# A graph network's adjacency build on one core: the prologue reordered, count masks in bf16, node features loaded and split earlier

## The chip, the cores and the metric

The kernel runs on one core of a Trainium2 chip. The metric is the time of one execution in microseconds of device time, the median over several runs. The engines are TensorE (PE in the rows; PEld is its weight load), VectorE (DVE), ScalarE (ACT), GpSimd (POOL) and SyncE (SP), which issues most DMAs. Each engine works through its own instructions in order and waits on semaphores for the others.

## The reference

Four graph layers follow one another on 3125 nodes with 128 features and 53125 edges sorted by destination; each ends in a residual sum and a layer norm. The change touches what goes before the first one and the walk that the other three use:

```python
src = jnp.concatenate([_s, _d, _loop])
dst = jnp.concatenate([_d, _s, _loop])
_o = jnp.argsort(dst, stable=True)
...
for l in range(N_LAYERS):                      # first graph layer, 4 rounds
    agg = jax.ops.segment_sum(x[src], dst, num_segments=n)
    h = x + agg
    h = jnp.maximum(h @ W1[l] + b1[l], 0.0)
    x = h @ W2[l] + b2[l]
```

## The kernel before

**Stages.** The kernel turns the edge list into a dense matrix `adj` (nodes by nodes, counts in bf16), so that the four rounds of `segment_sum` become matmuls (the dense layers). The other three graph layers gather rows by edge with indirect DMAs (the gather passes). The stages stand one after the other: prologue, build of `adj`, dense layers, tables and gather passes.

**Prologue.** The edges are cut into 416 tiles of 128. The *fine walk* has 620 steps, each a pair of a tile and a block of 16 destination nodes that it reaches; the *coarse walk* has 440 steps over blocks of 128. VectorE loads the last destination of each tile (`tmax`), compares it with a row of step numbers (`fcmp_m`, `cmp_m`, L1587 and L1588), and TensorE counts the ones with a matmul against `ones` (L929, L932): that gives each step's tile (`fts_f`, `ts_f`). From them VectorE makes selection masks (`fsel_m`, `sel_m`, L1597 and L1600), with which TensorE picks the tiles' destinations and sources (L937, L945); these become `drel`, and the comparison keys `fkey` and `flow`. VectorE further works out, on one partition, the place of each step's sum and of its ring slot for the gather passes (`walk_i`, L1605 to L1616), the slots of the fine sums (`fslot_i`), the step at which each block ends (`ends_f`, turned by TensorE, L951, and read by ScalarE into `ends_i`), and a number `peak_i` which every engine loads and branches on: zero (always here) leads to the dense path. GpSimd's part are constants and a check on the coarse walk (`off_f`, and the copies `gwalk`, L767 to L772), for which VectorE waits before it sets `ends_ready`. L957 and L958 join sources and edge kinds into `tile8` and `tile16`.

**Build.** TensorE clears its eight banks (L971), waits for `peak_set`, branches, and runs 31 iterations of four groups of five fine steps. For each group VectorE writes one-hots (`fine_hots`: one L1676, five L1680; two buffers, so at most two groups ahead), TensorE multiplies them (L1001), and ScalarE copies each finished block of 16 columns into `adj` and clears its slot (`copy_out`, L1379 and L1383). From iteration 6 on TensorE adds to each group a part of the first round's sums over the features (L985), 20 iterations with 15 such matmuls each. In these iterations it needs `x3`, the node features as a sum of three bf16 parts.

**Features.** `features_in_parts` on GpSimd (L886 to L900) makes `x3` from seven chunks of `x`, four instructions a chunk (the last is a quarter). It stands behind the branch on `peak_i`, and so do the DMAs of `x` (SyncE, L639 to L642), which land in columns of `adj` that the build reaches late (`xlate`, `xrem`). TensorE waits for them block by block in the first of its sums (`xparts_set`).

**Order.** Everything stands in the order in which it is written. In VectorE's code `link` adds a semaphore wait behind an instruction whose result the next needs. `walk_i` is read only in the gather passes, `gwalk` only where `peak_i` is above zero.

## Time and profile before

| | us |
|---|---|
| median of 3 runs | 2730.95 (2728.96 to 2734.68) |
| the profiled execution, its own time | 2718.4 |
| its span, first to last instruction | 2716.5 |
| prologue, to the first L1001 | 0 to 74.57 |
| build, 31 iterations | 74.57 to 356.59 |

Mean granted TensorE clock of the span: 0.726. A row of the timeline gives start, duration, engine, line, operation, what is written and read, partitions x elements, a count of merged instructions, and in brackets how long the engine was idle before and what released it. An f32 matmul stands in the rows as two.

### The profile page before, as it was taken

What the parts mean: (1) busy time and instruction counts of PE and PEld (TensorE: products, weight loads), DVE (VectorE), ACT (ScalarE), POOL (GpSimd) and SP (SyncE); (2) the same over time, 40 slices, a digit from 0 to 9 for tenths busy, and PEclk for the clock granted to TensorE, in tenths of its full rate; (3) what the DMA queues carried; (4) which work ended last, traced back from release to release, by engine and by line L of the source; (5) the groups of instructions that cost most, each with busy time, mean ns of one, the idle gap of its engine ahead of it and who ended that gap; (6) DMA issues with size and microseconds to landing.
All of it is one profiled execution on the core that took longest, in us unless ns stands there. A gap on an engine that the chain in (4) does not pass through costs nothing.

```text
span 2716.5 us, 30629 instructions
## 1 busy us (share of the span) xinstructions
PE 1369.1 (50%) x6416; PEld 878.8 (32%) x6417; DVE 913.9 (34%) x2288; ACT 657.2 (24%) x1868; POOL 1353.2 (50%) x1570
## 2 busy tenths in 40 slices
PE   4578789999852444543453243443344223233323
PEld 3244344554432332332331232332233123122323
DVE  6777731211276222222233232322234012111212
ACT  0567720000121222332231233333334000000000
POOL 1300045303136666666644666666662756666665
PEclk8699999999885766766776566666767556565656
DMA  0000010000341222322222122222221211111111
GB/s 18 25 0 0 0 11 8 6 0 7 110 185 47 93 78 92 96 77 92 94 81 77 43 69 67 70 59 67 70 67 58 51 42 51 48 49 45 50 46 43
DMA packets 120575, 148.92 MB, mean 55 GB/s; under 512 B 74731, under 2 KB 88689, under 8 KB 117314
## 3 DMA queue, kind: packets, MB, share of 16 engines
q0 software_dynamic: 40000, 81.89, 11.6%
q1 hardware_dynamic: 80514, 66.31, 7.4%
q8 instruction: 27, 0.44, 0.1%
q14 instruction: 34, 0.28, 0.0%
HBM read 91.39 MB, written 56.72 MB: 55 GB/s over the span
## 4 chain that ended last, share of the span: by engine, by line
PE 33%; another core or an unknown queue 30%; issue 17%; DVE 10%; ACT 5%; DVEq 1%; POOL 1%; DMA 1%; ACTq 1%; SPq 0%; POOLq 0%
PE acc L1123 12%; PE acc L1270 9%; PE acc L1236 4%; PE acc L1001 3%; ACT adj L1460 3%; DVE feat L1680 2%; PE acc L1206 2%; DVE adj L1875 1%; ACT adj L1379 1%; POOL adj L837 1%; PE acc L1055 1%; PE acc L985 1%; DVE adj L1944 1%; DVE feat L1676 1%
## 5 line engine op out<-in xcount | busy, mean ns | idle before, releaser
L837 POOL DMA_INDIRECT adj<-table,adj x1248 | 1196.1, 958 | 724.9 <-issue 362.2
L1270 PE MATMUL acc<-adj 128*128 x2640 | 477.0, 346 | 457.5 <-issue 220.3
L1270 PEld LDWEIGHTS acc<-adj 128*128 128x128 f32 x2640 | 434.7, 252 | 514.4 <-issue 513.3
L1123 PE MATMUL acc<-adj,feat 128*128 (+1 forms) x1800 | 337.0, 348 | 2.2 <-DVE adj L1715 2.2
L1875 DVE TENSOR_TENSOR adj<-acc,drel 128x768 f32<-128x768 f32 (+1 forms) x148 | 138.6, 945 | 456.5 <-remote 304.2
L787 POOL TENSOR_TENSOR node_rep<-node_rep,compb 128x128 f32<-128x128 f32 x128 | 58.4, 456 | 464.6 <-DMA node_rep<-in_L_gnn_weight_dram 455.8
L1460 ACT ACTIVATE adj<-adj 128x128 f32<-128x128 f32 x832 | 259.3, 387 | 100.1 <-issue 70.1
L1223 PE MATMUL acc<-ident,adj 128*128 128x128 f32 x50 | 22.0, 439 | 487.4 <-DVE adj L1914 383.4
L1236 PE MATMUL acc<-adj 128*128 128x512 f32 (+2 forms) x400 | 201.7, 660 | 98.4 <-ACT adj L1475 67.9
L1443 ACT ACTIVATE adj<-feat 128x4 int32 (+1 forms) x196 | 34.2, 202 | 882.3 <-remote 635.0
L1123 PEld LDWEIGHTS acc<-adj,feat 128*128 (+1 forms) x1800 | 156.1, 98 | 176.3 <-issue 3.6
L1001 PE MATMUL acc<-feat 128*128 128x400 bf16 x620 | 143.3, 371 | 83.2 <-DVE feat L1680 33.8
L1223 PEld LDWEIGHTS acc<-ident,adj 128*128 128x128 f32 x50 | 8.6, 172 | 497.6 <-issue 301.2
L1680 DVE TENSOR_SCALAR feat<-feat,temp 128x400 bf16<-128x400 int16 x620 | 163.6, 330 | 0.0
L1236 PEld LDWEIGHTS acc<-adj 128*128 128x128 f32 x400 | 94.9, 265 | 188.1 <-issue 117.7
L1896 DVE TENSOR_TENSOR adj<-acc,adj 128x128 f32<-128x128 f32 x75 | 21.7, 289 | 332.4 <-remote 282.9
L1666 DVE TENSOR_TENSOR adj<-node_iob,drel 128x384 f32<-128x384 bf16 (+1 forms) x148 | 74.9, 551 | 171.6 <-remote 130.8
L1001 PEld LDWEIGHTS acc<-feat 128*128 128x128 bf16 x620 | 75.0, 121 | 155.9 <-issue 141.2
L1379 ACT ACTIVATE adj<-acc 128x400 f32 (+1 forms) x196 | 96.5, 493 | 86.2 <-PE acc L1001 82.0
L1443 ACT ACTIVATE adj<-tile 128x4 int32 (+1 forms) x98 | 17.6, 201 | 360.4 <-remote 306.1
L1383 ACT ACTIVATE acc<-zerob 128x400 f32<-128x400 bf16 x196 | 99.5, 508 | 18.0
L1676 DVE TENSOR_TENSOR feat<-node_rep,feat 128x640 bf16<-128x640 bf16 x124 | 74.1, 598 | 75.4 <-PE acc L1001 66.1
(262 smaller groups left out, 1149.6 us busy)
## 6 DMA issues: line engine op xcount, KB each, us to landing
table<-adj SPq DMA_DIRECT2D x50, 512.0 KB
table<-adj SPq DMA_DIRECT2D x25, 1024.0 KB
adj<-table,adj POOLq DMA_INDIRECT x1250
table<-adj SPq DMA_DIRECT2D x25, 64.0 KB
adj<-in_x_dram SPq DMA_DIRECT2D x3, 512.0 KB, 6.4
out_dram<-adj SPq DMA_DIRECT2D x24, 64.0 KB
wrel<-node_rep SPq DMA_DIRECT2D x16, 64.0 KB, 3.0
adj<-in_L_gnn_W_dram SPq DMA_DIRECT2D x2, 512.0 KB
```

The costliest lines, as they stand in the source:

```text
L837: pool.indirect_dma_start(ring[:, p_, 0:D], None, table, bass.IndirectOffsetOnAxis(ap=gidx[:, p_:p_ + 1], axis=0)).then_inc(msgs_in[u.r][c ...
L1001: nc.tensor.matmul(acc[:, bass.ds(places[q * FG + j], FCOLS)], flo[:, q % FBUF, :, j], foh[:, q % FBUF, j, :], start=False, stop=True, ski ...
L1123: last = nc.tensor.matmul(acc[:, c * KB:c * KB + chunk(c)], x3[:, s, bass.ds(b, 1), :].rearrange("p b f -> p (b f)"), adj[:, bass.ds(b, 1) ...
L1236: nc.tensor.matmul(o, xT1[:, b.r, :], table, start=True, stop=True).then_inc(prod_full[j], 1)
L1270: last = nc.tensor.matmul(acc[:, bass.ds(blk[s], width)], hot[:, c, j, :], ring_flat[:, bass.ds(place[s], width)], start=False, stop=True, ...
L1379: nc.scalar.activation(adj[:, :, bass.ds(i * (TURN * FB) + r * FB, FB)], fslots[r % FSLOTS].rearrange("p (h n) -> p h n", n=FB), ACT.Copy) ...
L1383: nc.scalar.activation(fslots[r % FSLOTS], zerob[:, 0:FCOLS], ACT.Copy).then_inc(zeroed, 1)
L1460: last = nc.scalar.activation(o, o, ACT.Copy, scale=WEIGHT[ph][:, bass.ds(tiles_from(u, c) + j, 1)])
L1666: return nc.vector.tensor_tensor(o, node_iob[:, :].unsqueeze(1).to_broadcast([P, n, P]), drel[:, bass.ds(s, n)].unsqueeze(2).to_broadcast( ...
L1676: nc.vector.tensor_tensor(flo[:, q % FBUF, :, :], node_iof[:, :, :], flow[:, bass.ds(m * FPI + (at_ * FPI + q * FG), FG)].unsqueeze(1).to_ ...
L1680: last = nc.vector.tensor_scalar(foh[:, q % FBUF, j, :], col_io, fkey[:, bass.ds(m * FPI + (at_ * FPI + q * FG + j), 1)], None, ALU.is_equal)
L1875: last = nc.vector.tensor_tensor(hot[:, c, 0:n, :], psum_bank(IOTA_BANK)[:, 0:P].unsqueeze(1).to_broadcast([P, n, P]), drel[:, bass.ds(t.n ...
```

## The change

- `fcmp_m`, `cmp_m` and the matrix of ones they are multiplied with become bf16 (`ones_b`, with a memset of its own). The matmul of the fine counts releases VectorE by itself, the coarse one after it.
- VectorE's prologue is written in another order: what leads to `ends_ready` first (`fts_f`, `fsel_m`, `bs_f`, `fclamp`, `until`, the three maxima), then `fslot_i`, then `drel` and the keys; `peak_i` is set in their midst rather than behind the first one-hots. The conversion and comparison of `later_f` move ahead of the wait for the counts.
- The places for the gather passes leave the prologue. `walk_rows` computes them from `gwalk` in place, in `walk_i`, in round 1 of the dense layers, between `merge` and `updates`.
- TensorE makes `tile8`'s product (`kinds_and_sources`) ahead of the selections, takes the fine selections before the coarse one, and clears six banks before it waits for `tiles_set`.
- `x` goes to memory of its own (`xu`, `xrem`), issued by SyncE right behind the edge lists and ahead of `compb`, `w1first` and the biases. GpSimd clears the last block of `xu` as its first instruction and splits chunks 0 to 2 before its check on the coarse walk, chunks 3 to 6 behind it. TensorE waits for all of `x3` before it sets `zeroed`; the waits in the loops go.

```diff
-        cmp_m = carve([TQ, TC, WSTEPS])
+        cmp_m = carve([TQ, TC, WSTEPS], BF16)
+        ones_b = carve([TQ, P], BF16)
-        fcmp_m = carve([TQ, TC, FW])
+        fcmp_m = carve([TQ, TC, FW], BF16)
+        xu = carve([P, BLOCKS, D])
+        xrem = carve([P, BLOCKS, D])
...
+            for i in range(3):
+                sp.dma_start(xu[:, 8 * i:8 * i + 8, :],
+                             x[8 * i * P:(8 * i + 8) * P].rearrange("(b p) f -> p b f", p=P)).then_inc(xu_in[i], 16)
+            sp.wait_ge(xtail_set, 1)
+            sp.dma_start(xu[0:LASTN, BLOCKS - 1, :], x[(BLOCKS - 1) * P:N]).then_inc(xu_in[3], 16)
             sp.dma_start(compb[:, :, :], g2comp.partition_broadcast(P)).then_inc(comp_in, 16)
...
+            nc.gpsimd.memset(xu[:, BLOCKS - 1, :], 0.0).then_inc(xtail_set, 1)
...
+            def features_in_parts(chunks):
+                for c in chunks:
+                    pool.wait_ge(xu_in[c // 2], 16)
+                    nc.gpsimd.tensor_copy(p0, u).then_inc(xsplit, 1)
+                    pool.wait_ge(xsplit, 3 * c + 1)
+                    nc.gpsimd.tensor_tensor(rem, u, p0, ALU.subtract).then_inc(xsplit, 1)
+                    pool.wait_ge(xsplit, 3 * c + 2)
+                    nc.gpsimd.tensor_copy(p1, rem).then_inc(xsplit, 1)
+                    pool.wait_ge(xsplit, 3 * c + 3)
+                    nc.gpsimd.tensor_tensor(p2, rem, p1, ALU.subtract).then_inc(xparts_set, nb)
+
+            features_in_parts(range(0, SPLIT_FIRST))
             pool.wait_ge(bs_set, 1)
             pool.wait_ge(off_set, 4)
...
+            features_in_parts(range(SPLIT_FIRST, CH))
             pool.wait_ge(comp_in, 16)
...
-            pe.wait_ge(walk_set, 2)
-            pe.wait_ge(tiles_set, 2)
-            pe.wait_ge(ends_set, 3)
-            clear_sums(8)
+            pe.wait_ge(ends_set, 3)
+            pe.wait_ge(walk_set, 2)
+            clear_sums((0, 1, 2, 5, 6, 7))
+            pe.wait_ge(tiles_set, 2)
+            clear_sums((3, 4))
+            pe.wait_ge(xparts_set, BLOCKS)
             pe.nop(nofuse=True)
             pe.sem_inc(zeroed, FSLOTS)
...
             def layers(general):
                 for l in range(LAYERS):
                     if l < LAYERS - 1:
                         merge(l)
+                    if l == 1 and not general:
+                        walk_rows()
```

Where VectorE stood in the program between the coarse walk and the start of the fine slots before:

```order
L1603 TENSOR_TENSOR adj<-adj 128x620
L1605 TENSOR_SCALAR walk_i<-adj 1x24x3 [waits setup_dve]
L1607 TENSOR_SCALAR walk_i<-adj 1x2
L1609 TENSOR_SCALAR adj<-adj 1x450
L1610 TENSOR_SCALAR adj<-adj 1x450
L1611 TENSOR_SCALAR adj<-adj 1x900 [waits setup_dve]
L1612 CAST adj<-adj 1x900 [waits setup_dve]
L1613 SCALAR_TENSOR_TENSOR adj<-adj 1x450 [waits setup_dve]
L1614 SCALAR_TENSOR_TENSOR adj<-adj 1x450
L1615 TENSOR_SCALAR walk_i<-adj 1x25x18 [waits setup_dve]
L1616 TENSOR_SCALAR walk_i<-adj 1x25x18
L1619 TENSOR_SCALAR adj<-adj 128x620
```

The same stretch of VectorE in the changed kernel, up to the instruction that sets `ends_ready` (L1633):

```order
L1615 TENSOR_TENSOR adj<-adj 128x450 [waits setup_dve]
L1617 TENSOR_SCALAR adj<-adj,tile_io 104x440 x4
L1619 TENSOR_TENSOR adj<-adj 128x620
L1621 TENSOR_SCALAR adj<-adj 128x620 [waits setup_dve]
L1622 CAST adj<-adj 1x620 [waits setup_dve]
L1624 TENSOR_SCALAR adj<-adj,part_io 128x620 x2
L1626 TENSOR_REDUCE peak<-adj 104x1 [waits setup_dve]
L1627 TENSOR_REDUCE ends_f<-adj 128x2
L1629 SCALAR_TENSOR_TENSOR adj<-adj 1x124
L1630 TENSOR_REDUCE peak_row<-adj 1x1 [waits setup_dve]
L1633 TENSOR_REDUCE peak_row<-adj 1x1 [waits gwalk_set,off_set,setup_dve]
```

The ten rows on one partition are gone, and `ends_ready` comes before the slots and the keys rather than behind them. GpSimd before, from its last constants to its branch:

```order
L762 MEMSET adj 1x2 [waits off_set]
L764 CAST adj<-adj 1x936 [waits off_set]
L767 TENSOR_TENSOR adj<-adj 1x440 [waits off_set,bs_set]
L768 TENSOR_TENSOR adj<-adj 1x440
L769 CAST gwalk<-adj 1x450
L770 CAST gwalk<-adj 1x450
L772 TENSOR_TENSOR adj<-adj 1x440 [waits off_set]
L481 TENSOR_LOAD peak_i [waits comp_in,peak_set]
```

And in the changed kernel, from its third chunk of the features to the first instruction of the fourth:

```order
L776 CAST feat<-adj 128x512 [waits xu_in1]
L778 TENSOR_TENSOR adj<-adj,feat 128x512 [waits xsplit]
L780 CAST feat<-adj 128x512 [waits xsplit]
L782 TENSOR_TENSOR feat<-adj,feat 128x512 [waits xsplit]
L787 TENSOR_TENSOR adj<-adj 1x440 [waits off_set,bs_set]
L788 TENSOR_TENSOR adj<-adj 1x440
L789 CAST gwalk<-adj 1x450
L790 CAST gwalk<-adj 1x450
L792 TENSOR_TENSOR adj<-adj 1x440 [waits off_set]
L776 CAST feat<-adj 128x512 [waits xu_in1]
```

Twelve splitting instructions now stand ahead of the check on which `ends_ready` waits, sixteen behind it. TensorE before, from the last product of sources and kinds to the branch:

```order
L957 MATMUL acc<-adj 128x104
L958 MATMUL acc<-ident,adj 128x104
L971 MATMUL acc<-zerob 128x512 [waits ends_set,tiles_set,walk_set]
L971 MATMUL acc<-zerob 128x512 x7
L481 TENSOR_LOAD peak_i [waits peak_set]
L1353 COMPARE_AND_BRANCH
```

And in the changed kernel:

```order
L945 MATMUL acc<-adj 128x104
L946 MATMUL acc<-ident,adj 128x104
L983 MATMUL acc<-zerob 128x512 [waits walk_set,ends_set]
L983 MATMUL acc<-zerob 128x512 x5
L983 MATMUL acc<-zerob 128x512 [waits tiles_set]
L983 MATMUL acc<-zerob 128x512
L483 TENSOR_LOAD peak_i [waits xparts_set,peak_set]
L1364 COMPARE_AND_BRANCH
```

The load of `peak_i`, behind which the build begins, has `xparts_set` as a further condition.

## Rows read from the trace of the kernel before

**Rows 1.** Chain of waits around the start of the build (start, us, what).

```profile
67.19 7.38 issue
74.57 1.87 PE acc L1001 x5
```

**Rows 2.** Busy time by stretch: PE, PEld, DVE, ACT, POOL, granted clock, DMA, GB/s.

```profile
74.57:103.77 29.20, 13.86 (x40) 5.41 (x41) 26.91 (x46) 12.57 (x26) 24.35 (x27) 0.56 0.02 5
103.77:137.25 33.48, 21.91 (x81) 10.34 (x81) 27.47 (x99) 24.21 (x51) 0.00 (x0) 0.77 0.00 0
137.25:316.12 178.87, 145.50 (x700) 76.60 (x701) 135.03 (x485) 122.70 (x256) 0.00 (x0) 0.98 0.00 0
```

**Rows 3.** Timeline of VectorE: one group beside the split, one after it.

```profile
84.68 1.50 DVE L1676 TENSOR_TENSOR feat<-node_rep,feat 128x640 bf16<-128x640 bf16 x1
...
86.11 2.93 DVE L1680 TENSOR_SCALAR feat<-feat,temp 128x400 bf16<-128x400 int16 x5
...
105.78 0.56 DVE L1676 TENSOR_TENSOR feat<-node_rep,feat 128x640 bf16<-128x640 bf16 x1 [1.27 <-PE acc L1001]
106.25 1.25 DVE L1680 TENSOR_SCALAR feat<-feat,temp 128x400 bf16<-128x400 int16 x5
```

**Rows 4.** Timeline of GpSimd: check, chunks of the split, its end.

```profile
27.55 1.60 POOL L767 TENSOR_TENSOR adj<-adj 1x440 f32<-1x440 f32 x1 [21.38 <-DVE adj L1602]
...
31.60 1.48 POOL L772 TENSOR_TENSOR adj<-adj 1x440 f32<-1x440 f32 x1
...
73.39 0.61 POOL L894 CAST feat<-adj 128x512 bf16<-128x512 f32 x1 [2.75 <-DMA adj<-in_x_dram]
...
77.15 0.94 POOL L894 CAST feat<-adj 128x512 bf16<-128x512 f32 x1
...
81.44 0.94 POOL L894 CAST feat<-adj 128x512 bf16<-128x512 f32 x1
...
100.25 0.55 POOL L900 TENSOR_TENSOR feat<-adj,feat 128x128 bf16<-128x128 f32 x1
```

**Rows 5.** Timeline of VectorE in the prologue.

```profile
12.44 0.96 DVE L1591 CAST adj<-adj 104x1536 f32<-104x1536 int32 x1
22.23 0.63 DVE L1593 COPY adj<-acc 128x450 f32<-128x450 f32 x1 [8.83 <-PE acc L932]
...
27.39 0.80 DVE L1603 TENSOR_TENSOR adj<-adj 128x620 f32<-128x620 f32 x1
28.21 1.02 DVE L1605 TENSOR_SCALAR walk_i<-adj 1x72 int32<-1x72 f32 x1
...
35.33 0.60 DVE L1616 TENSOR_SCALAR walk_i<-adj 1x450 int32<-1x450 f32 x1
...
53.26 0.60 DVE L1661 TENSOR_REDUCE peak_row<-adj 1x1 f32<-1x440 f32 x1
```

**Rows 6.** Timeline of TensorE in the prologue: counts, clearing of banks.

```profile
12.58 6.58 PE L929 MATMUL acc<-adj,ones 104*128 104x310 f32 x16 [12.58 <-DVE adj L1588]
...
63.46 3.57 PE L971 MATMUL acc<-zerob 128*128 128x512 bf16 x8 [1.96 <-issue]
```

**Rows 7.** SyncE's queue: first of the small weights, and the features.

```profile
6.37 0.36 SPq L596 DMA_DIRECT2D compb<-in_L_gnn_comp_dram  x1
...
67.98 3.63 SPq L639 DMA_DIRECT2D adj<-in_x_dram  x3
```

**Rows 8.** Timeline of TensorE in a build iteration with sums, slow and fast groups.

```profile
146.31 1.59 PE L1001 MATMUL acc<-feat 128*128 128x400 bf16 x5 [1.93 <-ACT acc L1383]
147.69 1.49 PE L985 MATMUL acc<-adj,feat 128*128 x3
...
152.63 1.04 PE L1001 MATMUL acc<-feat 128*128 128x400 bf16 x5
...
157.70 0.81 PE L985 MATMUL acc<-adj,feat 128*128 x3
```

**Rows 9.** Timeline of VectorE in round 1 of the dense layers.

```profile
475.33 0.69 DVE L1768 TENSOR_TENSOR temp<-acc,l0c 128x512 f32<-128x512 f32 x1 [11.33 <-PE acc L1055]
```

More of the change, by code:

```diff
@@ L250, in gnn @@
         assert used[0] <= BLOCKS * NA // 2
-        late = big.rearrange("p (h w) -> p h w", h=BLOCKS)
-        xlate, xrem = (late[:, :, LATE_COL + i * D:LATE_COL + (i + 1) * D] for i in range(2))
         used[0] = 0
@@ L401, in gnn @@
         splitting = sem("splitting")
[L402 removed]
+        xl_in = sem("xl_in")
+        xu_in = [sem(f"xu_in{i}") for i in range(4)]
+        xtail_set = sem("xtail_set")
         xsplit = sem("xsplit")
```

189 lines of the change are left out of this document (91 added, 98 removed).

## The prediction

> **What bounds the kernel now.** I read the chain of waits first, then the busy time by stretch, then the timelines of the engines before 75 us. The stages follow one another, and nothing in them is tied to an absolute time, so what the prologue or the build gives up moves the end by as much. The build begins with the first L1001 at 74.57; ahead of it the chain shows 7.38 us of "issue" since `peak_set` at 67.19 [rows 1]: TensorE loads `peak_i`, branches and loads the registers of its loop. Since GpSimd starts the split only after the same signal, its chunks lie under the first two of 31 iterations, which take 29.20 us; the next four take 33.48, or 8.37 each [rows 2]. The 20 iterations with sums have TensorE busy for 145.5 of 178.9 us [rows 2]. In the prologue VectorE is the chain: it waits 8.83 us for the counts and then works nearly without a gap from 22.23 to 53.86 [rows 5].
>
> **The start of the build.** It comes 7.4 us [rows 1] after the last of three things: `peak_set` (VectorE), `xparts_set` (GpSimd) and the cleared banks (TensorE). I take each alone, then together.
>
> *VectorE alone.* The f32 counts run from 12.58 to 22.2 [rows 5, 6], 24 entries for 12 matmuls. In bf16 the eight fine ones have 2480 columns; a bf16 group of 5x400 columns takes 1.87 us at the slow pace [rows 1], so 2.3 us, and VectorE goes on at 14.9 instead of 22.2: 7.3 us gained. The coarse ones need 1.7 us more and are ready at 16.6, while VectorE makes `fsel_m`. The masks' own cost does not change, I assume (SBUF to SBUF either way). From 22.23 to 53.86 are 31.6 us of work. The places for the gather passes (28.21 to 35.93) take 7.7 of them [rows 5]. The comparison of `later_f`, 1.2 us, moves into the wait for the counts. The last four key instructions, some 2.6 us, now stand behind `peak_set`; the cast of `node_iof` and the two instructions that make `peak_i` add 0.9. That leaves 31.6 - 7.7 - 1.2 - 2.6 + 0.9 = 21.0, and `peak_set` at 14.9 + 21.0 = 35.9. The new memsets (`ones_b`, `xu`) cost 0.2 or less.
>
> *GpSimd alone.* `x` is issued where `compb` was, at 6.37, and took 67.98 to 73.39 from issue to use, 5.4 us [rows 4, 7]; behind the edge lists I put it at 12.5. The three issues take 3.63 us of SyncE [rows 7] and push back `compb`, `w1first` and the biases, which nobody wants before the build is over; SyncE then waits for `peak_set` as before. A chunk alone takes 77.15 - 73.39 = 3.76, beside VectorE 81.44 - 77.15 = 4.29; the whole split took 27.4 (to 100.80), of which five chunks were the slower kind, so alone 27.4 - 5 x 0.53 = 24.8 [rows 4]. The check takes 27.55 to 33.08, 5.5 us [rows 4]. Together 30.3, and the last part is ready at 12.5 + 30.3 = 42.8.
>
> *TensorE.* The fine selections (8.5 us of work) and the coarse ones fit ahead of VectorE's later steps, at half pace too. Clearing takes 3.57 [rows 6] and begins when `drel` is made, some 5 us ahead of `peak_set`. It ends 1 to 2 us before `peak_set` and costs nothing; without that cover it would cost its last banks, about 1 us.
>
> *Together.* This is the term that decides. While a chunk is split, a VectorE group of one L1676 and five L1680 takes 1.50 + 2.93 (4.29 from start to start) where it takes 0.56 + 1.25 afterwards [rows 3]. It shows elsewhere too: L1605, 72 numbers on one partition, takes 1.02 us and ends just as GpSimd's instruction does at 29.15, and that instruction took 1.60 because it started beside L1603 [rows 4, 5]. So the two engines take turns, one instruction each or two short ones. In the new prologue VectorE has 32 instructions between L1591 and the one that sets `peak_i` which read and write SBUF alone (no reduction, no PSUM), 16.6 us together by their present durations; GpSimd has 33 in the same time. From below: GpSimd loses 0.53 us for 1.67 us of VectorE's work, as in the chunks [rows 3, 4], so 16.6 x 0.53 / 1.67 = 5.3, ready at 48. From above: one after the other without overlap, 42.8 + 16.6 = 59.4. VectorE's instructions here are longer than in the groups (0.5 us against 0.3) and hide less in GpSimd's gaps, so I take a value between, nearer the row that shows one instruction of each kind in turn: 53. VectorE has as many turns to wait and the check in its way (`ends_ready` waits for it, behind twelve splitting instructions); it comes out at about the same 53. The two first one-hot groups follow at 57 to 59, under the 7.4 us.
>
> The shared access is where the Trainium skill speaks against the change. SBUF — State Buffer, § Who interferes with whom, states an exclusive lock: VectorE in a two-port mode, or with two SBUF inputs against a GpSimd instruction that reads SBUF, blocks GpSimd for the whole instruction and the other way round. The rows agree in kind: L1676 has two SBUF inputs and was stretched from 0.56 to 1.50 [rows 3]. By the rule taken literally the sum would be the 59.4 above, and the build would begin at 66.8 rather than at 60.4.
>
> So the first L1001 comes at 53 + 7.4 = 60.4, a gain of 74.57 - 60.4 = **14.2 us** (bounds: 42.8 + 7.4 = 50.2, a gain of 24.4, and 59.4 + 7.4 = 66.8, a gain of 7.8).
>
> **The first two iterations.** With the split over, they run like the next four: 29.20 - 2 x 8.37 = **12.5 us** gained [rows 2]. From below 10, if the slow pace of TensorE (granted clock 0.56 there, 0.77 in the next four [rows 2]) costs more than I see; from above 13.5.
>
> **What is moved or free.** `walk_rows` puts ten instructions, some 7 us by their rows here, and three waits into round 1. VectorE is idle there for 11.33 us up to the next L1768 at 475.33, and idles before each later chunk as well, while TensorE has sums to do [rows 9]: nothing. If GpSimd's weight slices stretched them past 11.3, some 1 to 3 us would eat into that later slack. The DMAs of `x` leave 67.98; whether they slowed the 7.38 us no row shows, between 0 and 2 us of further gain, taken as 0.
>
> **Sum.** 14.2 + 12.5 = 26.7 us. The profiled execution of 2718.4 would become 2691.7. It lies 12.5 under the median of the runs, 2730.95, against which I forecast: 2730.95 - 26.7 = **2704.3**.
>
> **The rivals.**
>
> *A lighter prologue.* Waits in VectorE's chain (for the counts, for the check) let GpSimd work unhindered and its gaps take the rest: `peak_set` and `xparts_set` at 43 to 48. For it: 0.53 us a chunk is all that GpSimd lost in the rows [rows 4]. Against it: there it met short instructions. Gain 19 to 24 at the start plus 12.5: 2694 to 2699.
>
> *A heavier one.* The lock held in full, or a check that comes late and leaves VectorE idle before `ends_ready` with all its keys still to do and sixteen splitting instructions to pass: 58 to 66 for `peak_set`. Gain 1 to 9 plus 12.5: 2709 to 2717.
>
> *The change doesn't do what it says at the start.* If neither the bf16 counts nor the order shortens the way to `peak_set`, only the split's absence from the build is left: 2730.95 - 12.5 = 2718.
>
> *The clock, on the other side.* In the iterations with sums the granted clock is 0.98, nearly all at the upper of its two levels, 2.4 GHz; in the first two it is 0.56, mostly at 1.2 GHz [rows 2]. At the lower level a group of L1001 takes 1.86 instead of 1.04 and three sums 1.49 instead of 0.81 [rows 1, 8], so an iteration of four groups and 15 sums loses 4 x 0.82 + 5 x 0.68 = 6.7 us. In the new kernel TensorE does less before the build. If that kept it at the lower level, four of the 20 iterations would cancel the gain and ten would make it 2731 + 40 = 2771. Against it: the level rose at the same place in the loop after a stretch at 0.56 in this trace as well, and the loop's own work is unchanged. TensorE: Matmul & The Clock Gate of the Trainium skill, § Part 1, ties the level to recent activity; by that rule the sums themselves bring it back, as the rows show.
>
> **How the numbers follow.** My forecast (2700 to 2708) has 0.55, the lighter prologue 0.17, the heavier 0.16, no gain at the start 0.05, the clock 0.05, of which half ends slower than before, and 0.02 are other things. A change under about 0.2% (5.5 us) can't be told from none here. So faster 0.94, same 0.03, slower 0.03. The range takes in the forecast, most of both neighbours and 3 us of scatter between runs: 2694 to 2715.
>
> **What would show it.** The first L1001 at 60 (57 to 65), with 7.4 us of "issue" behind the later of `peak_i` and the last splitting instruction; if it is 67 or later, my price of turns is too low. The fine counts in some 2.3 us, and VectorE's copy of them near 15. In the prologue VectorE's casts and scalar operations at 1.0 to 1.5 us beside GpSimd. The first two iterations in 16.7 us. From iteration 6 to the end of the build about 219 us as before, and the rest of the kernel unchanged to within 3 us; a difference there would make the forecast wrong for a reason that isn't in it.

## The result, and the profile after

The changed kernel takes 2692.81 us (median of 4 runs, 2688.71 to 2695.69) against 2731.89 (4 runs, 2728.96 to 2734.68) measured beside it: a ratio of 0.9864, 95% interval 0.985 to 0.9878. The forecast was 2704.3, the range 2694 to 2715: the direction was right, the gain larger than forecast (39 us instead of 26.7), and the median lies 1.2 us under the range. Its profiled execution took 2694.58 us, with a span of 2692.8; between the two profiled executions there are only 23.8 us (23.7 by their spans); the last experiment shows why.

Stage by stage, in the two profiled executions:

| stage | before, us | after, us | gain | forecast |
|---|---|---|---|---|
| to the first fine product | 74.57 | 54.49 | 20.1 | 14.2 |
| first two iterations | 29.20 | 16.98 | 12.2 | 12.5 |
| next four | 33.48 | 31.58 | 1.9 | 0 |
| 20 iterations with sums | 178.87 | 175.04 | 3.8 | 0 |
| rest, to the start of the last fine product | 37.93 | 38.66 | -0.7 | 0 |

The last fine product starts at 354.05 before and at 316.75 after: 37.3 us of gain, all of it made before the dense layers begin.

Busy time by stretch of the kernel after (PE, PEld, DVE, ACT, POOL, granted clock, DMA, GB/s), against [rows 2]:

```profile
54.49:71.47 16.98, 11.66 (x40) 5.26 (x41) 13.35 (x48) 12.05 (x26) 0.00 (x0) 0.74 0.00 0
71.47:103.05 31.58, 17.30 (x80) 9.58 (x81) 26.53 (x96) 24.43 (x51) 0.00 (x0) 0.95 0.00 0
103.05:278.09 175.04, 141.67 (x685) 75.95 (x701) 134.96 (x486) 122.60 (x256) 0.00 (x0) 1.00 0.00 0
```

GpSimd's column is 0.00 in the first row, where it was 24.35, and VectorE's is 13.35 where it was 26.91: the same groups without the split beside them. The granted clock is higher in each of these three rows than before.

Timeline of VectorE in the prologue of the kernel after (start, us, what); the last of them is the copy of the largest of the check that every engine branches on:

```profile
11.41 0.80 DVE L1600 TENSOR_SCALAR adj<-adj,tmax 104x450 bf16<-104x450 f32 x1
12.13 1.37 DVE L1599 TENSOR_SCALAR adj<-adj,tmax 104x620 bf16<-104x620 f32 x1
...
17.36 0.80 DVE L1608 COPY adj<-acc 128x620 f32<-128x620 f32 x1
18.20 3.44 DVE L1611 TENSOR_SCALAR adj<-adj,tile_io 104x620 f32<-104x620 f32 x4
...
47.20 0.14 DVE L1660 CAST peak_i<-peak 1x1 int32<-1x1 f32 x1
```

Timeline of GpSimd there, its first and last instruction of the split, and the first and last of the check between them:

```profile
10.98 0.98 POOL L776 CAST feat<-adj 128x512 bf16<-128x512 f32 x1 [4.67 <-DMA adj<-in_x_dram]
...
24.73 1.26 POOL L787 TENSOR_TENSOR adj<-adj 1x440 f32<-1x440 f32 x1
...
29.35 2.24 POOL L792 TENSOR_TENSOR adj<-adj 1x440 f32<-1x440 f32 x1
...
45.98 1.46 POOL L782 TENSOR_TENSOR feat<-adj,feat 128x128 bf16<-128x128 f32 x1
```

The two chains end together, VectorE's at 47.34 and GpSimd's at 47.44, and the first fine product follows 7.05 us behind. The clearing of the banks ended at 45.14. Timeline of TensorE, the bf16 counts (the fine ones, L934, are those that took 6.58 in [rows 6]) and the first fine products:

```profile
14.27 2.25 PE L934 MATMUL acc<-adj 104*128 104x310 bf16 x8 [14.27 <-DVE adj L1600]
16.31 1.71 PE L938 MATMUL acc<-adj 104*128 104x450 bf16 x4
...
54.49 3.52 PE L1015 MATMUL acc<-feat 128*128 128x400 bf16 x10 [9.35 <-issue]
```

The eight fine counts take 2.25 us (2.3 were forecast), but they begin at 14.27, and VectorE goes on at 17.36 instead of 14.9. Two of the reasons stand in VectorE's rows above: the masks L1599 and L1600, 0.54 and 0.45 us when alone, take 1.37 and 0.80 once GpSimd has begun at 10.98.

SyncE's queue: `x` at the place that `compb` had [rows 7], 4.6 us ahead of its first use on GpSimd.

```profile
6.38 2.72 SPq L599 DMA_DIRECT2D adj<-in_x_dram  x3
9.14 1.32 SPq L602 DMA_DIRECT2D adj<-in_x_dram  x1
```

Timeline of VectorE in round 1 of the dense layers, where the turn and ring places now are (against [rows 9]):

```profile
428.51 0.20 DVE L1793 TENSOR_SCALAR walk_i<-gwalk 1x72 int32<-1x72 int16 x1
...
432.38 0.59 DVE L1812 TENSOR_SCALAR walk_i<-walk_i 1x450 int32<-1x450 int32 x1
439.74 0.69 DVE L1766 TENSOR_TENSOR temp<-acc,l0c 128x512 f32<-128x512 f32 x1 [6.76 <-PE acc L1065]
```

The ten instructions take 4.5 us, and 6.76 us of idle time are left before VectorE is next wanted: they are free, as forecast.

### The profile page after: what moved, and what is told of

The parts are those of the page before. It is cut to its first block, busy times and chain, and to the rows that moved or that the text cites. A ratio compares the mean times of both kernels' runs of the same rounds, so it can differ in the third digit from the quotient of the medians.

```text
span 2692.8 us, 30484 instructions
## 1 busy us (share of the span) xinstructions
PE 1328.5 (49%) x6309; PEld 860.3 (32%) x6405; DVE 910.1 (34%) x2289; ACT 657.4 (24%) x1868; POOL 1355.7 (50%) x1570
## 4 chain that ended last, share of the span: by engine, by line
another core or an unknown queue 33%; PE 28%; issue 18%; DVE 11%; ACT 5%; DVEq 1%; POOL 1%; ACTq 1%; DMA 0%; SPq 0%; POOLq 0%
PE acc L1134 12%; PE acc L1281 6%; PE acc L1247 3%; PE acc L1015 3%; ACT adj L1471 2%; DVE adj L1902 2%; PE acc L1217 2%; DVE feat L1680 2%; ACT adj L1390 1%; PE acc L1065 1%; DVE adj L1971 1%; PE acc L999 1%; DVE adj L1925 1%; DVE adj L1927 1%
## 5 line engine op out<-in xcount | busy, mean ns | idle before, releaser
L1281 PE MATMUL acc<-adj 128*128 x2640 | 468.7, 342 | 538.3 <-issue 282.1
L1281 PEld LDWEIGHTS acc<-adj 128*128 128x128 f32 x2640 | 425.1, 248 | 546.4 <-issue 545.6
L1134 PE MATMUL acc<-adj,feat 128*128 (+2 forms) x1766 | 336.4, 349 | 4.0 <-DVE adj L1713 2.2
L1454 ACT ACTIVATE adj<-feat 128x4 int32 (+1 forms) x196 | 34.2, 202 | 894.2 <-remote 715.6
L1247 PE MATMUL acc<-adj 128*128 128x512 f32 (+2 forms) x400 | 195.4, 643 | 104.2 <-ACT adj L1486 104.2
L1015 PE MATMUL acc<-feat 128*128 128x400 bf16 x620 | 136.4, 357 | 75.9 <-ACT acc L1394 38.6
L1680 DVE TENSOR_SCALAR feat<-feat,temp 128x400 bf16<-128x400 int16 x620 | 155.4, 321 | 0.0
L1247 PEld LDWEIGHTS acc<-adj 128*128 128x128 f32 x400 | 92.1, 257 | 191.5 <-ACT adj L1486 108.1
L1417 ACT ACTIVATE feat<-acc,l0c 128x512 f32<-128x512 f32 (+1 forms) x28 | 16.0, 633 | 310.9 <-PE acc L1134 294.9
```

Source lines behind the costliest of these rows:

```text
L1015: nc.tensor.matmul(acc[:, bass.ds(places[q * FG + j], FCOLS)], flo[:, q % FBUF, :, j], foh[:, q % FBUF, j, :], start=False, stop=True, ski ...
L1134: last = nc.tensor.matmul(acc[:, c * KB:c * KB + chunk(c)], x3[:, s, bass.ds(b, 1), :].rearrange("p b f -> p (b f)"), adj[:, bass.ds(b, 1) ...
L1247: nc.tensor.matmul(o, xT1[:, b.r, :], table, start=True, stop=True).then_inc(prod_full[j], 1)
L1281: last = nc.tensor.matmul(acc[:, bass.ds(blk[s], width)], hot[:, c, j, :], ring_flat[:, bass.ds(place[s], width)], start=False, stop=True, ...
L1680: last = nc.vector.tensor_scalar(foh[:, q % FBUF, j, :], col_io, fkey[:, bass.ds(m * FPI + (at_ * FPI + q * FG + j), 1)], None, ALU.is_equal)
```

## The experiments

The first eleven ran where all times are lower: the kernel before takes 2439.22 us there (median of 9 runs; 2435.04, one run, beside the four experiments from the float32 masks to the split ahead, and 2439.85, 9 runs, beside the three after those) in place of 2731.89. From the last fine product to the end it is 2082 to 2088 us in all variants there, and 2376.1 here, so the difference lies in the stages that the change leaves alone; the prologue and the build have the same times on both. I call the time from the last fine product to the end "the rest". Five runs of one kernel lie up to 10 us apart (2397.96 to 2408.13 for the changed one), so an experiment with one run is read from its landmarks alone: the first fine product, iteration 6, the last fine product. The last of them has a scatter of its own, since the 20 iterations with sums take 2 us more in some profiles than in others, the repeated changed kernel among them (177.04 us against 175.04 in the first profile).

**The changed kernel again.** 

> The changed kernel itself once more, as the measure for the others. Both theories expect the first L1015 at 54.5 us within 1 us, peak_i and the last splitting instruction within 1 us of each other at 47 to 48, iteration 6 of the build at 103 within 2 us, and a ratio to the kernel before of 0.986 within 0.0015. If the start of the build moved by more than 2 us from one execution to the next, single profiles could not tell the other experiments apart.

Measured: 2401.0 us (2397.96 to 2408.13), ratio 0.9841 (0.9828 to 0.9854). First fine product 54.22, VectorE's `peak_i` done at 47.78, last part of the split at 46.45, iteration 6 at 102.97, last fine product 317.98. The two chains end 1.3 us apart, a little more than expected. It is the reference for what follows.

**No split at all.** The parts of `x` are zeros, written by ScalarE: the kernel leaves the features out of the first round's sums.

```
-            features_in_parts(range(0, SPLIT_FIRST))
...
-            features_in_parts(range(SPLIT_FIRST, CH))
```

> The changed kernel without the split of the features: GpSimd's 28 splitting instructions are left out, and ScalarE fills x3 with zeros, so the output is not the reference's. Theory A (VectorE and GpSimd take turns at their common access to memory, and that sets the start): VectorE's 21 us behind the counts run unhindered, the counts themselves are asked for 1.5 us earlier, peak_i is made at 36 to 38 and the first L1015 comes at 43 to 45, 10 us earlier than with the split. Rival B (the turns cost VectorE little, its chain of dependent instructions is what lasts until 47): peak_i at 45 or later and the first L1015 at 52 to 55. The check on GpSimd takes 5.2 to 5.7 us under both.

Measured: 2391.81 us (one run). Timeline of VectorE, the copy of the fine counts, the four selections behind it and `peak_i`, and of TensorE, the first fine product:

```profile
15.09 0.80 DVE L1600 COPY adj<-acc 128x620 f32<-128x620 f32 x1 [0.49 <-PE acc L917]
15.93 1.90 DVE L1603 TENSOR_SCALAR adj<-adj,tile_io 104x620 f32<-104x620 f32 x4
...
38.72 0.14 DVE L1652 CAST peak_i<-peak 1x1 int32<-1x1 f32 x1
```

```profile
45.26 3.53 PE L998 MATMUL acc<-feat 128*128 128x400 bf16 x10 [8.00 <-DVE feat L1672]
```

The first fine product comes at 45.26 and `peak_i` at 38.86, each 0.3 to 0.9 us later than theory A's range and far from rival B's. Without the split VectorE is 8.9 us faster to `peak_i` (38.86 against 47.78). That is the split's price for VectorE (GpSimd's check still runs beside it), and the price at the start of the build is 9.0 us. The counts are copied at 15.09, as I had worked out (14.9), so all of the delay to 17.36 came from the split.

**The split behind the branch, as before, and all else as after.** `x` is loaded and split behind `peak_set`, and TensorE waits chunk by chunk again.

```
-            features_in_parts(range(0, SPLIT_FIRST))
...
             hold(pool, peak_set, 1)
...
+                features_in_parts(range(CH))
```

> The changed kernel with the features' part undone: x is loaded behind the branch on peak_i (once the first two one-hot groups and tile8 and tile16 are made) into columns of adj, GpSimd splits it there during the build, and TensorE waits for it block by block. Masks in bf16, VectorE's new order and walk_rows stay. Theory A: the prologue loses its turns, the first L1015 comes at 43 to 46, but the build pays for the split again, about 12 us over its first iterations, so iteration 6 begins at 102 to 107 against 103, and the time is within 4 us of the changed kernel: what the split costs is paid in either place. Rival B (the prologue hides the split, the build doesn't): the first L1015 stays at 52 to 55 and iteration 6 begins at 114 to 117, 12 us slower in all.

Measured: 2410.54 us (2408.49 to 2414.51), ratio 0.9885 (0.987 to 0.99). Busy time by stretch, first two and next four iterations:

```profile
45.39:74.06 28.67, 13.57 (x40) 5.44 (x41) 26.78 (x43) 12.74 (x26) 23.09 (x24) 0.56 0.19 57
74.06:107.85 33.79, 20.93 (x81) 10.01 (x81) 29.41 (x101) 24.29 (x50) 2.69 (x5) 0.80 0.00 0
```

This is the cleanest of the comparisons: the same 29 us for two iterations as in [rows 2], after a prologue 29 us shorter. The build starts 8.8 us earlier than in the changed kernel and reaches iteration 6 at 107.85, 4.9 later. The split costs 9.0 us beside the prologue and 13.7 us beside the build (62.46 us for six iterations instead of 48.75), and the difference is what moving it brings, 4.9 us by iteration 6 and 7.1 by the last fine product (325.05 against 317.98). Of the further 2.2 us the 20 iterations with sums hold 1.9, at a clock that fell for a while in both profiles. The other 29.3 of the 34.2 us gained by iteration 6 come from the shorter way to the branch. I had expected iteration 6 by 107 and the totals within 4 us; the medians differ by 9.5.

This kernel also shows what the shorter way is made of, since like the kernel before it has no split beside its prologue. Timeline of VectorE, before, then here:

```profile
63.45 0.56 DVE L1676 TENSOR_TENSOR feat<-node_rep,feat 128x640 bf16<-128x640 bf16 x1 [9.17 <-issue]
...
67.03 0.14 DVE L1687 CAST peak_i<-peak 1x1 int32<-1x1 f32 x1
```

```profile
15.12 0.80 DVE L1615 COPY adj<-acc 128x620 f32<-128x620 f32 x1 [0.49 <-PE acc L938]
...
38.75 0.14 DVE L1667 CAST peak_i<-peak 1x1 int32<-1x1 f32 x1
```

`peak_i` is made 28.3 us earlier (38.89 against 67.17). VectorE goes on after the counts at 15.12 instead of 22.23, 7.1 us; the places took 7.6; and the largest part is the order. Before, VectorE was through with its prologue at 54.28, idled 9.17 us at the wait for `tiles_set` (TensorE's and ScalarE's work for `tile8` and `tile16`), wrote two one-hot groups and only then set `peak_i`: 12.9 us that are gone. No experiment undoes the order alone, so this part is read from the rows.

**The casts of the split on ScalarE.** GpSimd is left with 14 subtractions.

```
-                    nc.gpsimd.tensor_copy(p0, u).then_inc(xsplit, 1)
...
+                nc.scalar.activation(x3[:, s_, at_:at_ + nb, :], src_[:, at_:at_ + nb, :], ACT.Copy).then_inc(sem_, 1)
```

> The changed kernel with the two casts of each chunk made by ScalarE, which has nothing to do before 35 us; GpSimd keeps the two subtractions, 14 instructions instead of 28, and makes its check behind chunk 2 as before. Theory A: GpSimd's list falls from 30.3 to 14.9 + 5.5 = 20.4 us and VectorE has half as many turns to wait, so the last part is ready at 33 to 38 and peak_i at 39 to 43; the first L1015 comes at 46 to 50, 5 to 8 us earlier, and the time is 2685 to 2690. Rival B (the start hangs on VectorE's own chain): 54 as before and no change in time. Rival C: ScalarE's casts, which wait for GpSimd's remainders, hold up its reading of the maxima and with it peak_i; then the first L1015 comes later than 50 with VectorE waiting for ends_set.

Measured: 2400.53 us (2399.74 to 2405.74), ratio 0.9842 (0.9829 to 0.9856); first fine product at 53.78, where 46 to 50 were expected. GpSimd was done at 36.84, and VectorE's chain still ended at 46.91. It had no idle time at its wait for `ends_set`, so rival C isn't the reason. Timeline of VectorE, and of GpSimd's last subtractions:

```profile
11.41 1.31 DVE L1620 TENSOR_SCALAR adj<-adj,tmax 104x450 bf16<-104x450 f32 x1
12.64 1.37 DVE L1619 TENSOR_SCALAR adj<-adj,tmax 104x620 bf16<-104x620 f32 x1
...
33.87 2.70 DVE L1649 SCALAR_TENSOR_TENSOR adj<-adj 1x124 f32<-1x124 f32 x1
```

```profile
33.84 1.08 POOL L781 TENSOR_TENSOR feat<-adj,feat 128x512 bf16<-128x512 f32 x1
34.89 0.40 POOL L775 TENSOR_TENSOR adj<-adj,feat 128x128 f32<-128x128 f32 x1
35.25 1.59 POOL L781 TENSOR_TENSOR feat<-adj,feat 128x512 bf16<-128x512 f32 x2
```

L1649 handles 124 numbers on one partition and takes 0.36 us in the kernel without a split; here it lasts from 33.87 to 36.57, while the last subtractions of GpSimd run from 33.84 to 36.84 with no cast between them. Half the instructions of GpSimd gave VectorE 0.9 us back out of 8.9. So the number of GpSimd's instructions is not what VectorE pays by; what it does pay by, no run settles.

**Float32 masks and counts again.**

```
-        cmp_m = carve([TQ, TC, WSTEPS], BF16)
-        ones_b = carve([TQ, P], BF16)
...
-        fcmp_m = carve([TQ, TC, FW], BF16)
```

> The changed kernel with one part undone: the count masks and the row of ones are float32 again, the order of TensorE's count products stays. Theory A (the start of the build hangs on VectorE's chain, and the counts stand on it): the eight masks go back to the longer float32 form and the count products to TensorE's four passes, so the copy of the fine counts, at 18.6 us in the run of the changed kernel on this chip, falls back by 4 to 8 us, and the first fine product from 54.2 to 58 to 62 us. Rival B (the gain at the start is the split's early end alone, the counts lay beside it): the copy of the counts comes later, but the first fine product stays within 1 us of 54.2. Either way nothing behind the first fine product changes by itself, so iteration 6 of the build comes as much later as the first product does. Time: 4 to 8 us over the changed kernel by A, no difference by B.

Measured: 2404.93 us (one run), first fine product 57.25, last one 318.55. Timeline of TensorE:

```profile
15.54 7.49 PE L934 MATMUL acc<-adj 104*128 104x310 f32 x16 [15.54 <-DVE adj L1600]
22.86 3.19 PE L938 MATMUL acc<-adj 104*128 104x450 f32 x8
```

Timeline of GpSimd, the first instruction of its check:

```profile
27.46 1.25 POOL L787 TENSOR_TENSOR adj<-adj 1x440 f32<-1x440 f32 x1 [4.42 <-DVE adj L1615]
```

The fine counts take 7.49 us instead of 2.25, the copy of them comes 4.5 us later, and the build starts 3.0 us later. While VectorE waits 3.65 us for the counts, GpSimd finishes its first three chunks (at 23.04) and then idles 4.42 us for VectorE, whose four selections take 1.90 us in that time instead of 4.34: part of the delay is given back. Theory A in kind, a little under its range (58 to 62). The gain that I had booked for the counts, 7.3 us, is worth 3.0 at the start where a split fills the wait, and 2.7 at iteration 6. At the last fine product the two profiles are only 0.6 us apart, but there the repeated changed kernel has lost 2.3 us more in the 20 iterations with sums (177.04 against 174.73, at a granted clock of 0.99 against 1.00), which isn't a gift of the counts.

**The places back in the prologue.**

```
+            nc.vector.tensor_scalar(turn_i[0:1, 0, :], bs_f[0:1, :], 21846.0, None, ALU.mult)
...
-                    if l == 1 and not general:
-                        walk_rows()
```

> The changed kernel with the turn and ring places back in VectorE's prologue, behind the fine step numbers, and not in the dense layers. Theory A: the ten instructions on one partition cost their 7 to 8 us of the kernel before, or up to 13 us if each of them also waits for a GpSimd instruction of the split in progress (about 0.5 us each); GpSimd's split would be done ahead of the end of the chain. First fine product at 61 to 66 us instead of 54.2, the total later by as much. Rival B (GpSimd's split sets the start, VectorE has room beside it): GpSimd ends at 46 to 47 as before and the first fine product moves by less than 2 us. In the dense layers the 4.5 us of the moved rows lay before an idle time of VectorE of 6.8 us; by both theories taking them away gives less than 0.5 us there.

Measured: 2406.57 us (one run), first fine product 60.60, 6.4 us later (61 to 66 expected), last one 322.24. The ten instructions run from 29.25 to 37.61, 8.4 us, one of them on two numbers:

```profile
29.64 1.10 DVE L1625 TENSOR_SCALAR walk_i<-adj 1x2 int32<-1x2 f32 x1
```

It begins and ends with an instruction of GpSimd (29.61 to 30.72); in round 1, with GpSimd idle, the same work takes 0.15 us. Theory A again, just under its range. The 7.7 us of the sum lie between the 8.4 of these rows and the 6.4 at the start; at iteration 6 the difference is 6.6, and the 4.3 at the last fine product hold the same slower 20 iterations of the repeated kernel.

**The place of the check among GpSimd's work.** One number, `SPLIT_FIRST = 3`, set to 0 (check first) and to `CH` (split first).

> The changed kernel with one number changed: no part of the split stands ahead of GpSimd's check of the walk (SPLIT_FIRST 0 instead of 3). Theory A (turns on a shared access, VectorE's count masks held up by the split that begins at 10.8): without GpSimd beside it VectorE reaches the copy of the fine counts at 15.1 us as in the kernel without a split (18.6 with it), so the check begins 3 to 5 us earlier, near 19 to 20, and ends near 25; then all 28 instructions of the split follow, 30 us alone and 33 to 37 beside VectorE: end at 56 to 62, and TensorE, which waits for the last part, begins the fine products 6.6 to 7.4 us later, at 63 to 69. Rival B (GpSimd is not what TensorE waits for, it hides in the build): start below 54. Theory A's time: 9 to 15 us over the changed kernel.

> The changed kernel with one number changed: the whole split stands ahead of GpSimd's check of the walk (SPLIT_FIRST 7). Theory A: the split runs from 10.8 without a gap and is done at 41 to 46 us (30 alone, 35 beside VectorE); the check then takes 6 us, to 47 to 52; VectorE waits for it with its largest of the check, which was at 35.1, and what stood behind that one until the first fine product (19.2 us in the changed kernel, 16 to 17 without the split beside it) follows: first fine product at 63 to 69. Rival B (VectorE's chain has room against GpSimd's check): first fine product at most 2 us later than 54.2. Time by A: 9 to 15 us over the changed kernel.

Measured: 2409.92 and 2409.22 us (one run each); first fine product at 60.69 and 60.72, last one at 322.66 and 323.08. Both lose 6.5 us at the start, less than I had expected (63 to 69). Timeline of GpSimd with the check first, first and last instruction of the split:

```profile
24.93 1.76 POOL L776 CAST feat<-adj 128x512 bf16<-128x512 f32 x1
...
53.41 0.54 POOL L782 TENSOR_TENSOR feat<-adj,feat 128x128 bf16<-128x128 f32 x1
```

And with the split first, the first of the check, and the instruction of VectorE that waits for it:

```profile
38.01 0.41 POOL L782 TENSOR_TENSOR feat<-adj,feat 128x128 bf16<-128x128 f32 x1
38.38 1.10 POOL L787 TENSOR_TENSOR adj<-adj 1x440 f32<-1x440 f32 x1
...
41.52 1.10 POOL L792 TENSOR_TENSOR adj<-adj 1x440 f32<-1x440 f32 x1
```

```profile
42.72 0.60 DVE L1633 TENSOR_REDUCE peak_row<-adj 1x1 f32<-1x440 f32 x1 [6.55 <-POOL adj L792]
```

All 28 instructions take 29.0 us in the one and 27.9 in the other, beside a VectorE that works nearly all the time: GpSimd loses 3 to 4 us on the 24.8 that I had put for it alone (an estimate; no run has the split with VectorE idle). These rows price GpSimd's side of the term of the forecast that failed. With the check first TensorE waits for the split (53.95, then 6.74 us), with the split first VectorE idles 6.55 us for the check; 3 of 7 chunks ahead of it come nearest to a balance among the three that were run. With the check first VectorE makes `peak_i` at 44.09, 5.2 us later than without a split: it pays less where less of the split lies beside it.

**GpSimd waits for the masks** (casts on ScalarE as above).

```
+            pool.wait_ge(sel_ready, 2)
             features_in_parts(range(0, SPLIT_FIRST))
```

> The kernel with the casts of the split on ScalarE, and GpSimd waits with its first part until VectorE has made all count masks and copied the index rows (a wait on the count of selections, 2). Theory A (what the split costs at the start is the VectorE instructions that stand in its way, the masks above all): the masks and copies run as without a split and the copy of the fine counts starts at 15.1 to 16.5 us instead of 19.7 (18.6 in the changed kernel); GpSimd ends near 40, still ahead; the end of VectorE's chain (the copy of the largest of the check, 46.8 without the wait) moves to 42 to 44.5, and the first fine product, 6.6 to 7 us behind it, from 53.8 to 49 to 51.5. Time 2 to 5 us under the changed kernel. Rival B (the split's later start only moves the waits to other VectorE instructions, the number of GpSimd instructions decides): copy of the counts earlier, but the chain still ends at 46 or later and the first product stays within 1 us of 53.8.

Measured: 2402.77 us (2400.88 to 2403.76), ratio 0.9851 (0.9838 to 0.9865); first fine product 52.71, where 49 to 51.5 were expected. Timeline of VectorE:

```profile
15.41 0.81 DVE L1629 COPY adj<-acc 128x620 f32<-128x620 f32 x1
16.25 5.32 DVE L1632 TENSOR_SCALAR adj<-adj,tile_io 104x620 f32<-104x620 f32 x4
```

The copy of the counts comes at 15.41, 4.3 us earlier than in the kernel with ScalarE's casts (19.73), as theory A says, and then the four selections behind it take 5.32 us where they took 1.90 there: of 4.3 us there are 0.65 left at `peak_i` (46.26). That is rival B's outcome: the waits move to the next instructions that stand in the way. Its ground, the number of GpSimd's instructions, had fallen with ScalarE's casts. My theory that the masks were the costly ones falls too.

**The largest of the check copied earlier**, with the wait and the casts of the last kernel, and alone.

```
+            dve.wait_ge(ends_set, 1)
+            nc.vector.tensor_reduce(peak[0:1, 1:2], peak_row[:, :], AXX, ALU.max)
             dve.wait_ge(walk_ps, 3)
...
+            nc.vector.tensor_copy(peak_i[0:1, 0:1], peak[0:1, 1:2]).then_inc(peak_set, 1)
             dve.wait_ge(walk_ps, 4)
```

> As the kernel before it (casts on ScalarE, GpSimd waits for the masks), and VectorE takes the largest of the check and copies it to the register's row ahead of the source and difference rows (before its relative rows) instead of between them, so that the branch that every engine takes on it no longer stands behind seven further instructions. TensorE can begin the branch once its banks are cleared, some 4 us behind the relative rows. Theory A (TensorE's 6.6 to 7.2 us from the copy of the largest to the first fine product run from that copy or from the clearing, whichever is later, and VectorE's one-hot rows, first ready 4.5 us behind that copy, are not the bound): first fine product 1.5 to 3 us earlier than with the gate alone, 46.5 to 49.5. Rival B (the one-hot rows or the clearing bound it as late as the branch): no earlier than the gate alone, within 0.7 us.

> The changed kernel with the largest of the check taken and copied ahead of the relative rows and nothing else. TensorE still waits for the last part of the split (46.5 us on this chip, 47.6 for the copy of the largest). Theory A: two chains end within 1.2 us of each other here, so with the copy at 42 the first fine product can come at most 1.2 us earlier, at 53.0 to 53.5 instead of 54.2; time within 1.5 us of the changed kernel. Rival B (the branch is waited for alone, the split's end isn't on the chain): first fine product at 51 to 52.5, where the one-hot rows are ready.

Measured: together 2400.93 us (2397.49 to 2402.78), ratio 0.9838 (0.9825 to 0.9852), first fine product 50.83; alone 2406.22 us (2401.58 to 2406.87), ratio 0.9864 (0.9849 to 0.9879), first fine product 53.57. For the first 46.5 to 49.5 were expected; it is 1.9 us earlier than with the wait alone, within the 1.5 to 3 of theory A, but the kernel that it starts from was later than I had thought. Timeline of the first, VectorE's first one-hot rows and TensorE, and of TensorE in the second:

```profile
49.34 1.25 DVE L1701 TENSOR_SCALAR feat<-feat,temp 128x400 bf16<-128x400 int16 x5
```

```profile
50.83 3.52 PE L1024 MATMUL acc<-feat 128*128 128x400 bf16 x10 [4.89 <-DVE feat L1701]
```

```profile
53.57 3.52 PE L1015 MATMUL acc<-feat 128*128 128x400 bf16 x10 [6.93 <-issue]
```

Alone the early copy gains 0.65 us at the start: `peak_i` is ready at 42.37, and TensorE now waits for the split, which ends at 46.80, and begins 6.77 later. That shows that in the changed kernel both chains set the start. Together with the others the branch has vanished behind VectorE's one-hot rows, which are ready at 50.59; 3.4 us are won at the start and 3.4 at the last fine product (314.58), and the medians (2400.93 and 2401.0), taken at different times, don't show them. The second kernel's median is 5.2 us above the changed kernel's, where I had expected 1.5 at most, while its last fine product is 0.6 us earlier: the difference lies in the rest, or in the scatter. None of the variants that compute the whole result beats the changed kernel measurably.

**The kernel before, profiled again.** It ran where the first result was taken (2740.38 us beside it), not where the others did, so the numbers that it was to be held against are this table's and not those 2082 to 2088.

> The kernel before itself, profiled on the chip of the other experiments, where ten variants take 2082 to 2088 us from the last fine product to the end. Theory A (the whole gain is made by the end of the build; the 24 us between the two profiled executions understate the 39 us between the medians because the gather passes of before's execution were short by chance): first fine product at 74 to 75, last one 278 to 281 us later, at 353 to 355, and 2082 to 2089 us from there to the end, so a time of 2438 to 2446. Rival B (the places made in the prologue or the order of the dense layers cost or save something behind the build): more than 2092 or less than 2080 us from the last fine product to the end.

Measured: 2736.54 us; first fine product 74.34, last one 353.45. Busy time from the first product of the gather passes to the end, of the first profiled execution of before, of this one, and of the kernel after:

```profile
730.90:2716.50 1985.60, 768.67 (x3360) 569.86 (x3360) 575.94 (x1311) 443.42 (x1420) 1205.39 (x1275) 0.65 0.24 71
```

```profile
733.40:2734.70 2001.30, 751.11 (x3315) 564.90 (x3360) 577.59 (x1311) 443.68 (x1420) 1206.01 (x1275) 0.66 0.23 70
```

```profile
695.43:2692.80 1997.37, 744.68 (x3315) 557.53 (x3360) 577.66 (x1311) 443.76 (x1420) 1204.06 (x1275) 0.66 0.23 70
```

The same kernel has 1985.6 us in one execution and 2001.3 in the next for the same passes, with the same work on every engine: VectorE, ScalarE and GpSimd are busy for the same time within 2 us. TensorE's is 17.6 us less in the second, with 45 records fewer, as some of its records can be missing. The profiled execution of before was a short one there, and the kernel after lies between the two. From the last fine product to the end it is 2362.5 and 2381.2 us in the two profiles of the kernel before, and 2376.1 in the one after. So the 23.7 us between the first two spans are 37.3 of gain less 13.6 in a rest that differs by 18.8 between two executions of the same kernel. The medians differ by 39.1 us here and by 38.2 where the others ran, so 37.3 of them are made before the dense layers. Rival B isn't needed for what is seen, but with this scatter one or two microseconds of it can't be ruled out.

## Why the prediction was right, and where it was too low

| step | forecast | measured |
|---|---|---|
| `x` at GpSimd | 12.5 | 10.98 |
| fine counts copied | 14.9 | 17.36 (15.09 with no split) |
| VectorE alone | 35.9 | 38.86 |
| both chains together | 53 | 47.34 and 47.44 |
| from there to the build | 7.4 | 7.05 (6.4 to 8.0 in the variants) |
| first two iterations | 16.7 | 16.98 (16.3 to 17.1) |
| places in the dense layers | free | free, 6.76 us of slack left |
| iteration 6 to the end of the build | 219 | 216 |

**The step that failed is "Together".** It gave 53 for both chains where they end at 47.4, which is its lower bound (48) and the rival of a lighter prologue (43 to 48); the first fine product at 54.49 lies outside the 57 to 65 that I had named for it. For VectorE 53 left 17.1 us of waiting behind the 35.9 alone, about the full length of its 32 instructions on SBUF (16.6), as if each stood in turn with one of GpSimd's. Against the kernel with no split its whole chain lost 8.5 us (47.34 against 38.86). By the rows the 32 lost 7.4 of it: most of them 0.05 to 0.9 us each (L1652 1.21 against 0.80, L1653 1.25 against 0.48), about ten nothing (L1619 0.79 in both), one was shorter. Three masks ahead of them lost 1.5, of which 0.5 fell into the wait for the counts. GpSimd took 36.5 us from first to last where I had 30.3, an estimate: it lost 6.2, near the 5.3 of the ratio in [rows 3, 4] and far from the 10.2 that I chose. The 1.5 us by which `x` came earlier is the rest. So I took a value in the middle of the two ends, on the ground that VectorE's instructions are longer here than in the build, and that ground was wrong: for GpSimd the ratio of the build very nearly carried over.

The Trainium skill's SBUF — State Buffer, § Who interferes with whom, states an exclusive lock for a whole instruction. The runs agree with it in kind: reads of PSUM and reductions kept their times beside GpSimd (L1627 1.43 with and without a split), the instruction on two numbers did not. The sum that I had made from it, one engine after the other, put the start at 66.8, 12.3 us too late. Such a lock keeps two instructions apart; how often they would have met, it doesn't say.

**The counts** gave less than their 7.3 us. Undone alone they cost 3.0, since in VectorE's wait GpSimd gets ahead and then stands out of the way of the selections. Beside no split VectorE did go on 7.1 us earlier (15.12 against 22.23). VectorE without the split was 3.0 us slower than I put it, and the check is at least part of that: beside it the four L1609 of the kernel without a split take 3.54 us, where the wider L1603, alone, take 1.90. The forecast had the 13 us between VectorE's last prologue row and `peak_set` fall away without naming them as a term; they are the largest part of the shorter way, and they did.

**The first two iterations** were right to 0.3 us, and the kernel with the late split shows the cause: with it they take 28.67 us, where they take 17.04 in the repeated run.

**What was not in the forecast** are 5.0 us in the rest of the build (1.9, 3.8 and -0.7), nearly half of the excess; "Together" is the other half. The 3.8 us are TensorE's granted clock. Busy time of the second ten microseconds from the start of iteration 6, before and after:

```profile
147.25:157.25 10.00, 8.14 (x35) 3.95 (x34) 6.72 (x24) 5.82 (x12) 0.00 (x0) 0.86 0.00 0
```

```profile
113.05:123.05 10.00, 8.20 (x41) 4.52 (x42) 7.63 (x28) 7.09 (x15) 0.00 (x0) 1.00 0.00 0
```

In before's profile part of them is at the lower of the two levels, and TensorE has 35 instructions recorded where it has 41 after. TensorE is busy for 145.50 us with the 20 iterations before and 141.67 after, and the 3.8 us between them are the whole difference of the stage. The other two terms are of the size by which the changed kernel and its variants differ among themselves: 31.5 to 32.9 us for the four iterations ahead, 37.4 to 38.7 for the rest, longer at the lower clock for the most part. In all three profiles with the split beside the first iterations (before twice, and the late split) the stage takes 178.87 to 179.34; in the eleven others it takes 174.7 to 177.0. The clock kept low by a shorter prologue, my rival on the other side, did not come: the stage was not slower in any of them. Whether the split causes the dips through the slower start of the loop or whether they fall by chance isn't settled: three of the eleven have a dip too (the repeated one and the two with the early copy, 0.78, 0.83 and 0.83 in their first ten microseconds), for 1.5 to 2.0 us; the other eight take 174.7 to 175.2.

## What to carry to other kernels

Where two engines share access, a sum of both chains is an upper bound only: here GpSimd lost 6.2 us on an estimated 30.3 and VectorE 8.5 on 38.9, and the number of instructions didn't tell it. Look for what stands ahead of the signal that everyone branches on without being needed for it: that order was worth 12.9 us, more than the counts (7.1) or the places (7.6). Work moved beside a chain is best placed by the landmark that waits for both (the split's 13.7 us beside the build became 9.0 beside the prologue, with 3 of its 7 chunks ahead of the check, and would have been some 6.5 more with 0 or 7). And before two profiled executions are subtracted, compare a stage that the change leaves alone: here the gather passes differed by 12 us, a third of the gain, and by 16 between two executions of the same kernel.

## What the runs showed of the hardware

- VectorE's loss to GpSimd hardly fell with the number of GpSimd's instructions: 8.9 us beside 28 of the split, 8.1 beside 14 subtractions, 7.4 when these also began 2.3 us later. Keeping some instructions clear only moved the loss to the next ones. It did fall, to 5.2, where the split began only at 24.93.
- Beside a run of GpSimd subtractions with no cast between them an instruction of VectorE on 124 numbers took 2.70 us, in three profiles; with casts between them it took 0.94 or less, and 0.36 with no split beside it.
- From the last condition of the branch to the first product of the loop it is 6.4 to 8.0 us in eleven profiles of the changed kernel and its variants, whichever engine came last (8.0 once, the next below is 7.1), and it can be covered: with the copy for it 4.3 us earlier, TensorE began 0.24 us behind the first one-hot rows.
